# Stage 4 attention: scores formed by query and again by key in 32-row tiles

## The reference, cut to what matters

```python
q = x @ Wq
xc = jnp.concatenate((mem, x), axis=1)
k, v = jnp.split(xc @ Wkv, 2, axis=-1)
q, k, v = (to_heads(q), to_heads(k), to_heads(v))
dots = jnp.einsum('bhid,bhjd->bhij', q, k) * scale
mask = j_idx > i_idx + mem_len
dots = jnp.where(mask[None, None], -jnp.inf, dots)
attn = jax.nn.softmax(dots, axis=-1)
out = jnp.einsum('bhij,bhjd->bhid', attn, v)
return out.transpose(0, 2, 1, 3).reshape(b, n, dim) @ Wout + bout
```

## Time and profile before

| | |
|---|---|
| median of 3 runs | 904.66 us (904.29 to 908.63) |
| profiled execution, its own time | 906.1 us |
| its span, first to last instruction | 904.3 us |
| TensorE matmul busy | 826.6 us, 91% |
| VectorE / ScalarE / GpSimd busy | 538.3 / 438.3 / 91.7 us |
| mean granted TensorE clock | 0.977 |

### The profile page before, as it was taken

How to read it: one execution, slowest core, us unless ns; L and a number is a source line. 1 busy time by engine, 2 the same in 40 slices (tenths; PEclk the granted TensorE clock), 3 DMA queues, 4 the chain that set the end, 5 groups by cost and what they waited for, 6 DMA issues and landing times.

```text
span 904.3 us, 16120 instructions
## 1 busy us (share of the span) xinstructions
PE 826.6 (91%) x6069; PEld 411.9 (46%) x6069; DVE 538.3 (60%) x1205; ACT 438.3 (48%) x775; POOL 91.7 (10%) x74
## 2 busy tenths in 40 slices
PE   7999999997999779999967689999999989999997
PEld 4444444535555433343344454646555533443332
DVE  1634233335888766655578846676766667655653
ACT  3637373635677632343322426565646434554454
POOL 1360303021000000000024440000000000000000
PEclk9999999998999989999979999999999999999998
DMA  9300000000000000000000000000000000000000
GB/s 367 162 1 1 1 0 1 0 2 1 1 2 0 3 0 0 1 0 0 1 1 1 0 0 1 3 1 3 0 0 1 2 1 0 0 1 1 12 12 24
DMA packets 2363, 13.78 MB, mean 15 GB/s; under 512 B 257, under 2 KB 257, under 8 KB 1665
## 3 DMA queue, kind: packets, MB, share of 16 engines
q1 hardware_dynamic: 2304, 13.00, 3.6%
HBM read 11.95 MB, written 1.05 MB: 14 GB/s over the span
## 4 chain that ended last, share of the span: by engine, by line
PE 72%; DVE 13%; ACT 7%; issue 7%; DMA 1%; POOL 0%; DVEq 0%; ACTq 0%; SPq 0%
PE bank L2058 8%; PE bank L1679 5%; PE bank L2069 4%; PE bank L2221 4%; PE bank L1905 3%; PE bank L2147 3%; PE bank L1717 3%; PE bank L2200 3%; PE bank L2157 3%; PE bank L1730 3%; PE bank L1921 3%; PE bank L1910 3%; PE bank L2078 2%; PE bank L117 2%; PE bank L2136 2%
## 5 line engine op out<-in xcount | busy, mean ns | idle before, releaser
L2058 PE MATMUL bank<-sb_arena 128*64 128x256 f32 x512 | 82.4, 404 | 1.1 <-DVE sb_arena L1373 1.1
L1679 PE MATMUL bank<-sb_xT,sb_arena 128*128 128x512 f32 (+1 forms) x128 | 61.6, 613 | 3.5 <-ACT sb_arena L576 2.5
L829 ACT ACTIVATE sb_arena<-bank 128x512 f32<-128x512 f32 x64 | 37.7, 595 | 54.2 <-PE bank L2069 54.2
L1384 DVE TENSOR_REDUCE sb_rowmax<-bank 128x4 f32<-128x512 f32 x64 | 44.1, 690 | 30.7 <-PE bank L2058 30.0
L576 ACT ACTIVATE sb_arena<-bank 128x512 f32<-128x512 f32 x64 | 37.4, 597 | 36.2 <-PE bank L1679 36.1
L991 DVE TENSOR_TENSOR sb_arena<-bank,sb_arena 128x512 f32<-128x512 f32 x32 | 22.1, 690 | 50.2 <-PE bank L1730 49.9
L833 ACT ACTIVATE sb_arena<-sb_arena 128x512 f32<-128x512 f32 x64 | 40.3, 630 | 21.6 <-DVE sb_arena L1390 21.6
L728 ACT ACTIVATE sb_arena<-bank 128x512 f32<-128x512 f32 x36 | 21.4, 596 | 55.9 <-PE bank L1905 54.3
L1390 DVE TENSOR_TENSOR sb_arena<-bank,sb_rowmax 128x512 f32<-128x512 f32 x64 | 44.2, 691 | 2.5
L490 POOL TENSOR_TENSOR sb_arena<-sb_la,sb_consts 128x1024 f32<-128x1024 f32 x16 | 30.5, 1920 | 110.5 <-PE bank L1717 88.8
L2069 PE MATMUL bank<-sb_consts,sb_arena 128*128 128x128 f32 x256 | 40.9, 285 | 0.0
(11 more groups left out here) (333 smaller groups left out, 1681.7 us busy)
## 6 DMA issues: line engine op xcount, KB each, us to landing
sb_w<-w SPq DMA_DIRECT2D x1, 2646.5 KB, 27.0
sb_consts<-consts SPq DMA_DIRECT2D x1, 2236.0 KB, 14.3
sb_w<-w SPq DMA_DIRECT2D x1, 1736.0 KB, 20.2
sb_w<-w SPq DMA_DIRECT2D x1, 1175.0 KB, 8.3
sb_arena<-w SPq DMA_DIRECT2D x2, 512.0 KB, 4.2
sb_ctxT<-ctx SPq DMA_DIRECT2D x1, 1024.0 KB, 16.4
out<-sb_xT SPq DMA_DIRECT2D x4, 256.0 KB, 2.2
sb_xT<-x SPq DMA_DIRECT2D x1, 768.0 KB, 9.7
```

The costliest lines, as they stand in the source:

```text
L829: act.activation(probT4[k % 2][:, u % 4].rearrange("p j n -> p (j n)"), bank[2 + u % 2][:], ACT.Copy).then_inc(s_pt4, 1)
L1384: dve.tensor_reduce(rowmax4[u % 2][:], bank[(5, 0, 1)[u % 3]][:].rearrange("p (j t) -> p j t", j=4), AX, ALU.max).then_inc(s_mx4, 1)
L1679: pe.matmul(bank[h % 2][:], KT[:, h, :], cols(c), start=True, stop=True).then_inc(s_v, 1)
L2058: mm = pe.matmul(scored[64 * b:64 * b + 64, :, SEQ * half:SEQ * half + SEQ], qg4[:, g, q:q + SEQ], kx4[:, 2 * k + b, :, SEQ * half:SEQ * h ...
```

## The change

Scores are formed twice, in tiles of 32 rows, where group g lies in rows 32g to 32g + 31 of the array; a product there needs no zeros for the other groups, and different groups can be in different row tiles.

By query, `scores(k, half)`: two groups at a time, one in bank 0 and one in bank 1, with a bf16 mask added behind them from 32-row tiles. VectorE takes only the maxima of them (two reductions per half), and `split` writes the 16 maxima of a k as a high and a low bf16 part into `max4`. TensorE turns that tile (`turn`, one bf16 transpose into bank 7), ScalarE copies it to `maxT4`. By key, `scores_by_key(k)`: the same scores with keys on partitions, each group in a row tile and a bank of its own (2, 3, 5, 6), with masks; `less_max(k)` subtracts the maxima there by 16 bf16 products. ScalarE's `exps` then reads the banks and writes `probT4` directly. The subtraction on VectorE, `prob4`, the 64 transposes of a chunk and their copies are gone. q is scaled once (`q4`) and laid out by head (`qx4`), k is also copied whole (`k4`). Constants arrive packed as bf16 where they are used so, so that five conversions on VectorE at the start, and two at the start of stage 5, are gone. The logits of the next stage's router move from bank 6 to bank 7.

The lines that it takes away in `front4` are in the listing above; the diff here shows mostly what is new.

```diff
+    ident_bf = const_bf("ident_bf")
...
+    probT4 = [take(4 * CHUNK).rearrange("p (g b j q) -> p g b j q", g=4, b=2, j=4) for _ in range(2)]
     attn4 = take(CHUNK)
     xcat = take(2 * CHUNK).rearrange("p (b i t) -> p b i t", b=SEQS, i=2)
+    q4 = take(CHUNK)
+    qx4 = take(4 * CHUNK).rearrange("p (b j q) -> p b j q", b=SEQS, j=4)
+    k4 = take(SEQS * P).rearrange("p (b t) -> p b t", b=SEQS)
...
+    turned4 = bank[7][:, 0:SEQ].bitcast(BF16)
+    by_key = [bank[n] for n in (2, 3, 5, 6)]
...
@@ ACT, pre4 @@
+                src = bank[7 * n][:].rearrange("p (b t) -> p b t", b=4)
                 for j in range(4):
-                    act.activation(kx4[:, 4 * n:4 * n + 4, j, :], bank[n][:].rearrange("p (b t) -> p b t", b=4), ACT.Copy,
-                                   scale=const("inner")[:, j:j + 1]).then_inc(s_kx4, 1)
+                    act.activation(kx4[:, 4 * n:4 * n + 4, j, :], src, ACT.Copy, scale=const("inner")[:, j:j + 1])\
+                       .then_inc(s_kx4, 1)
+                wait(act, s_t4, 16 * c)
+                act.activation(k4[:, 4 * n:4 * n + 4, :], src, ACT.Copy).then_inc(s_kx4, 1)
...
@@ ACT, front4 @@
+            def exps(k):
+                wait(act, s_pv4, 4 * c + k - 1)
+                for g in range(4):
+                    wait(act, s_t4, 16 * c + 4 * k + g + 1)
+                    act.activation(probT4[k % 2][:, g].rearrange("p b j q -> p (b j q)"), by_key[g][:], ACT.Exp).then_inc(s_e4, 1)
+            def maxima_copy(k):
+                wait(act, s_tm4, 4 * c + k + 1)
+                wait(act, s_t4, 16 * c + 4 * k - 4)
+                act.activation(maxT4[k % 2], turned4, ACT.Copy).then_inc(s_mt4, 1)
+            for i in range(4 + 1):
                 if i == 2:
+                    hook(2)
+                if i >= 1:
+                    exps(i - 1)
+                if i < 4:
+                    maxima_copy(i)
+                if i == 1:
                     hook(1)
...
@@ DVE, pre4 @@
+            if piece == 1:
                 wait(dve, s_q4, c + 1)
-                wait(dve, s_s4, 16 * c)
-                for g in range(4):
-                    dve.tensor_scalar(qg4[:, g, :], bank[5][:], const("group")[:, g:g + 1], None, ALU.mult).then_inc(s_qg4, 1)
+                wait(dve, s_s4, 8 * c)
+                wait(dve, s_qx4, 5 * c)
+                dve.tensor_scalar(q4, bank[1][:], 8.0 ** -0.5, None, ALU.mult).then_inc(s_qx4, 1)
+            if piece == 2:
+                wait(dve, s_qx4, 5 * c + 1)
+                wait(dve, s_t4, 16 * c)
+                for j in range(4):
+                    dve.tensor_scalar(qx4[:, :, j, :], q4.rearrange("p (b q) -> p b q", b=SEQS), const("inner")[:, j:j + 1],
+                                      None, ALU.mult).then_inc(s_qx4, 1)
...
@@ DVE, front4 @@
+                for piece in range(3):
+                    pre4(0, piece)
+            def maxima(k, half):
+                wait(dve, s_s4, 8 * c + 2 * k + half + 1)
+                wait(dve, s_mb4, 4 * c + k - 1)
+                for n in range(2):
+                    g = 2 * half + n
+                    dve.tensor_reduce(rowmax4[k % 2][:, 4 * g:4 * g + 4], bank[n][:].rearrange("p (j t) -> p j t", j=4), AX,
+                                      ALU.max).then_inc(s_mx4, 1)
+            def split(k):
+                high, low = max4[:, k % 2, :, 0:4], max4[:, k % 2, :, 4:8]
+                top = rowmax4[k % 2][:].rearrange("p (g j) -> p g j", g=4)
+                if is_first(c) and k == 0:
+                    dve.wait_ge(s_z4, 2)
+                wait(dve, s_mx4, 16 * c + 4 * k + 4)
+                wait(dve, s_tm4, 4 * c + k - 1)
+                dve.tensor_copy(high, top).then_inc(s_hi4, 1)
+                wait(dve, s_hi4, 4 * c + k + 1)
+                dve.tensor_tensor(low, top, high, ALU.subtract).then_inc(s_mb4, 1)
...
+            for i in range(4 + 2):
+                if i < 4:
+                    maxima(i, 0)
+                    if i == 1 and not is_first(c):
+                        hook(0)
+                    if i == 3 and not is_first(c):
+                        hook(3)
+                    maxima(i, 1)
+                    split(i)
+                if i == 4:
+                    nxt(1)
+                if i >= 2:
+                    divided(i - 2)
+                if i == 4:
+                    nxt(2)
+                if i == 2:
                     hook(1)
                     nxt(0)
...
@@ PE, pre4 @@
-                for n in range(2):
-                    wait(pe, s_sb4, 16 * c - 2 + n)
-                    pe.matmul(bank[n][:], w(4, "wk"), xcat[:, 4 * n:4 * n + 4].rearrange("p b i t -> p (b i t)"),
-                              start=True, stop=True).then_inc(s_k4, 1)
-                wait(pe, s_sb4, 16 * c)
-                pe.matmul(bank[5][:], w(4, "wq"), cols(c), start=True, stop=True).then_inc(s_q4, 1)
+                wait(pe, s_mx4, 16 * c)
+                pe.matmul(bank[0][:], w(4, "wk"), xcat[:, 0:4].rearrange("p b i t -> p (b i t)"),
+                          start=True, stop=True).then_inc(s_k4, 1)
+                pe.matmul(bank[1][:], w(4, "wq"), cols(c), start=True, stop=True).then_inc(s_q4, 1)
             if piece == 1:
-                wait(pe, s_pt4, 16 * c)
+                if is_first(c):
+                    wait(pe, s_resid, 4 * NCH)
+                wait(pe, s_mt4, 4 * c)
+                pe.matmul(bank[7][:], w(4, "wk"), xcat[:, 4:8].rearrange("p b i t -> p (b i t)"),
+                          start=True, stop=True).then_inc(s_k4, 1)
+            if piece == 2:
+                wait(pe, s_e4, 16 * c)
...
@@ PE, front4 @@
+                for piece in range(3):
+                    pre4(0, piece)
+            def rows(g):
+                return slice(32 * g, 32 * g + 32)
+            def scores(k, half):
+                groups = (2 * half, 2 * half + 1)
+                wait(pe, s_kx4, 10 * c + 5 * (k // 2) + 5)
+                wait(pe, s_qx4, 5 * c + 1)
+                wait(pe, s_mx4, 16 * c + 4 * k + 2 * half)
+                for part in range(2):
+                    at = slice(SEQ * part, SEQ * part + SEQ)
+                    for g in groups:
+                        scored = bank[g % 2][:].rearrange("p (j t) -> p j t", j=4)
+                        for b in range(2):
+                            q = (2 * k + b) * SEQ
+                            mm = pe.matmul(scored[64 * b:64 * b + 64, :, at], q4[rows(g), q:q + SEQ], kx4[rows(g), 2 * k + b, :, at],
+                                           start=(part == 0), stop=True, skip_group_check=(part == 1))
+                for g in groups:
+                    scored = bank[g % 2][:].rearrange("p (j t) -> p j t", j=4)
                     for b in range(2):
+                        for h in range(2):
+                            o = 64 * b + 32 * h
+                            mm = pe.matmul(scored[o:o + 32, :, SEQ:], eye32[rows(g)],
+                                           late_key[rows(g), h].unsqueeze(1).to_broadcast([32, 4, SEQ]), start=False, stop=True,
+                                           skip_group_check=True)
                 mm.then_inc(s_s4, 1)
+            def scores_by_key(k):
+                wait(pe, s_qx4, 5 * c + 5)
+                wait(pe, s_e4, 16 * c + 4 * k)
+                if k == 0:
+                    wait(pe, s_vx4, 8 * c + 8)
+                for b in range(2):
+                    for g in range(4):
+                        pe.matmul(by_key[g][:, 256 * b:256 * b + 256], k4[rows(g), 2 * k + b, :],
+                                  qx4[rows(g), 2 * k + b].rearrange("p j q -> p (j q)"), start=(b == 0), stop=True, skip_group_check=(b == 1))
+                for h in range(2):
+                    for g in range(4):
+                        o = 64 + 32 * h
+                        pe.matmul(by_key[g][o:o + 32, :].rearrange("p (a q) -> p a q", q=SEQ), eye32[rows(g)],
+                                  early_query[rows(g), h].unsqueeze(1).to_broadcast([32, 8, SEQ]), start=False, stop=True,
+                                  skip_group_check=True)
+            def less_max(k):
+                wait(pe, s_mt4, 4 * c + k + 1)
                 for j in range(4):
+                    for g in range(4):
+                        mm = pe.matmul(by_key[g][:].rearrange("p (b j q) -> p b j q", b=2, j=4)[:, :, j, :],
+                                       neg_head[rows(g), j, :], maxT4[k % 2][rows(g), :].rearrange("p (b q) -> p b q", b=2),
+                                       start=False, stop=True, skip_group_check=True)
+                        if j == 3:
+                            mm.then_inc(s_t4, 1)
+            def turn(k):
+                wait(pe, s_mb4, 4 * c + k + 1)
+                if k == 0:
+                    wait(pe, s_kx4, 10 * c + 10)
+                if k == 1:
+                    wait(pe, s_resid, 4 * NCH + c)
+                if k == 2:
+                    wait(pe, s_lnv, 4 * NCH + c)
+                if k == 3:
```

(27 more changed lines are left out.)

176 lines of the change are left out of this document (44 added, 132 removed).

## The result

| | before | after |
|---|---|---|
| median of 9 runs | 908.62 us (904.29 to 911.32) | 913.66 us (909.57 to 921.21) |
| span of the profiled execution | 904.3 us | 911.1 us |
| mean granted TensorE clock | 0.977 | 0.932 |
| VectorE / ScalarE busy | 538.3 / 438.3 us | 494.6 / 403.6 us |

The changed kernel takes 1.0078 times as long (95% interval 1.0048 to 1.0108; the ratio is taken over all runs, the two medians alone give 1.0055). The forecast was 876 us, with a range of 863 to 897.

A forecast was written before the change was run, and what follows sets the result against it. TensorE was taken to bound stage 4. Shorter chunk spans and an earlier start gain 2 x 8.1 + 7.4 + 1.0 + 8.0 = 32.6 us, less 4 for the clock: 904.66 - 28.6 = 876 us, range 863 to 897.

The forecast's parts named there:

- half of scores by query, masks with it: Stage 4 on TensorE: 16 passes in four tiles plus 8 mask products in eight tiles, 1.23 us per half.
- scores by key with masks: Stage 4 on TensorE: 16 passes in four row tiles plus 8 masks in eight tiles, 1.33 us per k.
- one k in all: TensorE work added for two sequences: 4.31 us, against 7.87 us removed, so 3.56 less per k.
- waits of round 0: TensorE idle 1.45 us between the halves of scores, then 1.85 us before the transpose for two reductions and the split.
- waits of rounds 1, 3 and end: TensorE idle 1.5 us before round 1's transpose, 1.0 before round 3's second scores, 0.6 for the division.
- constants: Five conversions leaving VectorE at the start and a smaller load of constants: no gain taken, between nothing and 2 us possible.
- middle chunk: Span between first scores of neighbouring middle chunks in stage 4: 38.8 us against 46.9, of which 6.4 us waits.
- the clock: Falls of TensorE's granted clock in stage 4, plus register steps in the loop: about 1 us a chunk, 4 us.
- The walk: Round-by-round pricing of a chunk's TensorE work and waits in stage 4: 32.6 us gained in all before the give-back.
- row tiles overlap only in part: Rival: only two row tiles run at once, keyed scores take 1.71 us, not 0.85; 895 us in all; chance 0.18.
- What I give back: Stage 4: one clock fall of 1.7 us in two chunks, plus register steps, 4 us off the gain, net 28.6.
- The clock stays low: Rival: clock low through rounds 0 to 3 of each chunk, costing 15 us a chunk, 930 us; chance 0.03.

The follow-up runs named there:

- e10: Changed kernel with the previous chunk's last PV and v projection in round 0's waits, fillers in rounds 1, 3 and first chunk's round 0: 866.57 us, 0.9556.
- e5: Changed kernel with full-array fillers in the two waits of round 0 only, none in round 1: 898.54 us, 0.9908 of the kernel before.
- e3: Kernel before with only the change's constants, packed as bf16, without the conversions at the start of VectorE: 908.38 us, 1.0009.
- e9: Changed kernel with full-array fillers in the waits of rounds 0 and 1, and eight more in round 3's wait: 882.25 us, 0.9704.
- e12: Changed kernel with 21 eight-column full-array products in the first chunk's round 0 waits, ahead of the loop: 907.21 us, 1.0003.
- e1: Changed kernel with idle full-array bf16 products (fillers) in the three waits of rounds 0 and 1 of each chunk: 881.31 us, 0.9734.
- e2: Changed kernel with as many fillers as e1 in the same waits, each in one 32 x 32 tile: 902.49 us, 0.9969.
- e11: Kernel before with three TensorE waits added in each chunk's first rounds, around work on all 128 rows: 935.67 us, 1.0318.
- e7: Changed kernel reordered: previous chunk's last PV and v projection in round 0's waits, transposes behind next round's first scores, no fillers: 884.80 us, 0.9765.
- e4: Changed kernel with a chunk's v projection moved from the end of the chunk before to between round 0's halves: 906.17 us, 0.9979.

## Why the prediction was wrong

| step | forecast | measured at full clock |
|---|---|---|
| half of scores by query, masks with it | 1.23 | 1.25 (566.04 to 567.29) |
| scores by key with masks | 1.33 | 1.42 (557.41 to 558.83, e10) |
| subtraction / transpose | 0.32 / 0.20 | 0.33 / 0.16 |
| one k in all | 4.31 | 4.41 |
| waits of round 0 | 1.45, 1.85 | 1.51, 1.91 |
| waits of rounds 1, 3 and end | 1.5, 1.0, 0.6 | 1.50 (e5), 1.13 in the first chunk, 0.44 |
| start of first scores after k projection | 1.0 earlier | 1.2 earlier |
| constants | nothing | 1.0009 (e3) |
| middle chunk | 38.8 | 40.3 (e9, fillers in the waits) |
| **the clock** | 4 over the stage | about 28.9 (e12 less e9) |
| **loading of instructions** | not in the sum | 7.7 (after less e12) |

The walk was right within 1.5 us a middle chunk, and the gaps came where they were put. The rival "row tiles overlap only in part" was wrong: sixteen records of the keyed scores, in four row tiles, start 1.08 us before their masks (567.29 to 568.37), where it had 1.71 and a change of form. Over the stage the sum was 183.5 - 31.6 = 151.9 and 4.0 given back, 155.9. Measured was 194.4: the walk's 151.9, 5.9 more in the stage with the clock held (e9, 157.8; 1.1 to 1.9 a chunk, which I didn't split further), 28.9 and 7.7. What the fillers of e9 cost beyond the waits that they fill is in the 5.9, so the split between it and the clock's 28.9 is not exact.

**The failed step is "What I give back".** It took one row, a fall to 0.72 for 6 us, and counted one such fall in two chunks, 1.7 us each. That row stood among products on the whole array. In rounds 0 to 3 of the new order most products use tiles of 32 rows, and there the clock falls at the waits of round 0 and is at half for 17 to 27 us a chunk, in one fall or several. The difference of 28.9 us is 7.2 a chunk. The rival "The clock stays low" named the place, the rounds and the kind of loss, and got a chance of 0.03, "against it: from round 2 on TensorE has next to no gap". That argument failed: 24.65 of 26 us busy, clock 0.50. Its price, 15 us a chunk, was too high by a factor of two.

**The missing step is loading of instructions.** TensorE's loop body grows from 353 to 469 products (counted in the two kernels), and the prediction didn't price it. The Trainium skill (Runtime: NRT & Kernel Launch, "Instruction fetch mechanics") says that a taken branch to code outside the loaded pages waits for its page; the idle time without a releaser behind the loop's jump, and its going with 42 more instructions ahead of the loop, agree with it; that it is the load of a page no run shows. Without the stall the changed kernel is at 1.0003, no change, so it makes up the whole of the 0.8% by which the change was slower.

What is shown by runs: the clock is the larger loss (e1, e9); how much of the array the filling work uses counts (e1 against e2); waits around full-row work can bring a fall too (e11), and a single one among tiled work can (e5); where the code lies moves the ratio from 1.0078 to 1.0003 (e12). Only argued: that the low clock's length comes from the tiles. e11 and the changed kernel differ in more than tile size. In the changed kernel five of seven returns fall together with a product on the whole array (560.45 above is one) and the other two come right behind `pv`, but two such products passed at half clock (596.11, 607.32). Open: why equal waits bring a fall at one place and none at another (e11's last chunk, e4's second, round 3 of e1 and of the changed kernel). Not tried: tiled work in the changed order with no waits and no fillers.

## What to carry to other kernels

Work in small tiles saves TensorE time only as long as its clock holds: before cutting products into tiles, look at the waits among them (here falls came behind waits of 0.6 to 2 us) and price the case in which the work behind them runs at half clock; here that was 7.2 us a chunk. Fill such waits first with full-row work that the kernel has anyway (22 us here, e7 against e12), then with fillers (18 us more, e10). When an edit makes a loop body longer, look for idle time without a releaser at its second pass and compare the instruction queue's packets.

## What the runs showed of the hardware that I had not expected

- The granted clock stayed 0.50 over 26 us in which TensorE was busy 24.65 us, in products of 32-row tiles; in e2 it was 0.50 with 6.00 of 6 us busy.
- Thirty fillers of 256 columns in three waits of a chunk held it at 1.00 through rounds 0 to 2 on the full array, and did not in one 32 x 32 tile, where it fell behind a rest of 0.55 us.
- Equal waits don't bring equal falls: 2.02 us in e4's second chunk with the scores behind it at full clock, 2.02 in the changed kernel's with 26 us at half.
- Twenty-one eight-column products on the full array, which left most of the waits idle, didn't hold it: at 546.26 in e12 the sixteen records have 1.98 us on the timeline, at full clock 1.09.
- Four row tiles run nearly fully at once: 16 f32 records of 256 columns, one at a time 3.41 us by the prediction's price, start 1.08 us before the masks behind them, where 0.85 and a change of form of 0.16 were reckoned. That is 3.2 times, or 3.7 by an estimate without that change. The Trainium skill (TensorE: Matmul & The Clock Gate, "Part 3: Packing small matmuls") has 3.07 times for four row tiles. Two row tiles by two column tiles take 1.02.
- 21 short products ahead of a loop removed 3.4 us of idle time inside it.
